# A DLRM tower on one core: the last tile's Gram matrix and first layer in two parts, and a later wait in the gather stream

## The reference

```python
combined = jnp.concatenate([dense_features[:, None, :], sparse_features], axis=1)   # (512, 27, 128)
interactions = jnp.einsum('bfd,bgd->bfg', combined, combined)
iu, ju = jnp.triu_indices(27, k=1)
z = jnp.concatenate([dense_features, interactions[:, iu, ju]], axis=1)
h = jnp.concatenate([z, dense_features], axis=1)          # 607 wide
h = jnp.maximum(h @ W_top1 + b_top1, 0.0)                 # 512
h = jnp.maximum(h @ W_top2 + b_top2, 0.0)                 # 256
y = h @ W_top3                                            # 1
```

## Time and profile before

| what | value |
|---|---|
| median of 3 runs | 140.15 us (139.18 to 140.3) |
| the profiled execution's own time | 141.27 us |
| its span, first to last instruction | 139.5 us |
| mean granted TensorE clock | 0.927 |
| TensorE busy | 116.3 us (83%) |
| VectorE, ScalarE busy | 79.1, 78.5 us |
| GpSimd busy | 69.8 us (50%) |

### The profile page before, as it was taken

The page is one execution under the profiler, slowest core; times in us unless marked ns, Lnnn a source line. Parts: engine busy times, 40 slices in busy tenths (PEclk is TensorE's granted clock), DMA queues, the critical chain, the costliest instruction groups (busy, mean ns, idle before and its releaser), DMA issues.

```text
span 139.5 us, 2681 instructions
## 1 busy us (share of the span) xinstructions
PE 116.3 (83%) x1038; PEld 97.9 (70%) x1038; DVE 79.1 (57%) x152; ACT 78.5 (56%) x157; POOL 69.8 (50%) x75
## 2 busy tenths in 40 slices
PE   0579999999999978783699876999559998929993
PEld 0347667667668646772699776999459997729992
DVE  3399999999999999397159212003931021860001
ACT  6985789699899861398159431232950312860021
POOL 2577570752783787676676775767767000000000
PEclk9999999999999999999569998699977999975799
DMA  4929767468698212121221221212212000000000
GB/s 145 259 56 276 234 162 215 136 146 250 155 341 269 55 38 56 42 56 45 62 63 42 59 66 40 56 42 56 61 38 56 19 0 7 0 0 5 0 0 1
DMA packets 6304, 12.58 MB, mean 90 GB/s; under 512 B 2545, under 2 KB 3157, under 8 KB 6163
## 3 DMA queue, kind: packets, MB, share of 16 engines
q1 hardware_dynamic: 3971, 7.68, 19.0%
q0 software_dynamic: 2176, 4.46, 12.3%
q10 hardware_dynamic: 144, 0.26, 0.7%
HBM read 11.27 MB, written 0.00 MB: 81 GB/s over the span
## 4 chain that ended last, share of the span: by engine, by line
DMA 36%; PE 31%; POOL 17%; issue 11%; DVE 4%; ACT 1%
DMA rows<-in_tbl_dram,ids_i 33%; POOL rows L336 17%; PE ps L595 16%; PE ps L566 4%; PE ps L606 4%; DVE z L480 4%; PE ps L517 3%; DMA ids_i<-in_ids_dram 2%; PE ps L550 2%; PE ps L616 1%; PE ps L614 1%; ACT y L423 1%; DVE h_t L489 0%
## 5 line engine op out<-in xcount | busy, mean ns | idle before, releaser
L336 POOL DMA_INDIRECT rows<-in_tbl_dram,ids_i x68 | 69.0, 1014 | 37.5 <-DMA rows<-in_tbl_dram,ids_i 20.0
L453 DVE TENSOR_SCALAR hot<-ps,row_no 125x512 fp32r<-125x512 f32 x54 | 36.6, 742 | 1.0 <-PE ps L504 1.0
L537 PE MATMUL ps<-hot,tab_lo 125*128 125x512 f32 x72 | 29.8, 414 | 1.7 <-DVE tab_lo L442 1.7
L534 PE MATMUL ps<-hot,tab_hi 125*128 125x512 f32 x72 | 30.5, 424 | 0.4 <-ACT emb_t L377 0.2
L480 DVE COPY z<-ps 32x112 f32<-32x112 f32 (+1 forms) x64 | 21.7, 340 | 12.2 <-PE ps L566 6.8
L404 ACT COPY z<-ps 32x112 f32<-32x112 f32 (+1 forms) x64 | 21.8, 341 | 11.8 <-PE ps L566 6.9
L566 PE MATMUL ps<-emb_t 128*64 128x52 f32 x512 | 18.2, 237 | 2.7 <-ACT emb_t L377 1.2
L566 PEld LDWEIGHTS ps<-emb_t 128*64 128x64 f32 x512 | 17.6, 154 | 3.9 <-ACT emb_t L396 2.0
L595 PE MATMUL ps<-z,w_pair 128*128 128x128 f32 (+1 forms) x112 | 17.9, 328 | 2.9 <-DVE z L480 2.9
L595 PEld LDWEIGHTS ps<-z,w_pair 128*128 128x128 f32 (+1 forms) x112 | 17.7, 244 | 3.3 <-ACT z L404 3.2
L411 ACT ACTIVATE h_t<-ps 128x128 f32<-128x128 f32 x16 | 4.3, 278 | 26.7 <-PE ps L595 26.7
(11 more groups left out here) (42 smaller groups left out, 88.8 us busy)
## 6 DMA issues: line engine op xcount, KB each, us to landing
tab<-in_tbl_dram SPq DMA_DIRECT2D x9, 448.0 KB
rows<-in_tbl_dram,ids_i POOLq DMA_INDIRECT x68, 2.6
w_fold<-w_pair SPq DMA_DIRECT2D x1, 1024.0 KB
w<-in_W_top_dram SPq DMA_DIRECT2D x1, 512.0 KB, 5.4
tab<-in_tbl_dram SPq DMA_DIRECT2D x9, 52.0 KB
x_rows<-in_r_dense_features_dram ACTq DMA_DIRECT2D x1, 256.0 KB, 3.1
w_x<-in_W_top_dram SPq DMA_DIRECT2D x1, 256.0 KB, 4.0
h_t<-in_W_top_dram SPq DMA_DIRECT2D x1, 256.0 KB, 4.4
```

The source lines that it names most:

```text
L336: pool.indirect_dma_start(out=rows[:, t, gathered.index(f), :], out_offset=None, in_=tables[f - 1], in_offset=bass.IndirectOffsetOnAxis(id ...
L453: nc.vector.tensor_scalar(hot[0:RP, k % OHB], ps[0:RP, IDV + n % 2, :], row_no[0:RP, c:c + 1], None, ALU.is_equal).then_inc(hot_dve, 1)
L534: nc.tensor.matmul(bank, tab_hi[0:RP, n % SPLIT, c], one_hot, start=c == 0, stop=False)
L537: nc.tensor.matmul(bank, tab_lo[0:RP, n % SPLIT, c], one_hot, start=False, stop=c == R8 - 1).then_inc(hot_used, 1)
```

## The change

Three things change together.

GROUPS is another partition of the same features: groups of 4, 4, 4, 3 and 3, in another order. The features 1, 2, 3 and 5, 6, 7 are now the last two groups. The wait of GpSimd stands ahead of a group's last gather, where it stood ahead of the second one.

For tile 3 (LAST) the Gram matrix is made in two parts, each over all 128 examples. The early part has the columns 8 to 25 (moving operand 36 wide), and it needs only the groups 0 to 2. The late part, the words v0 and v1 of ORDER, has the columns 0 to 7 (moving operand 16 wide), and it needs all. Each part has its own copies to z. The first layer of that tile is in two parts as well: mN does w_x and the five chunks of w_pair from column 8 up, and lN at the end the two chunks of columns 0 to 7. The four blocks then need four PSUM banks (block_ps). VectorE zeroes, with two more memsets before pads_ready, the slots of the features that the early part reads before they are there.

ORDER now gives a group's tile by name. The groups 3 and 4 of tile 3 go from the stage of tile 2 to the last stage. Of tile 0's groups ScalarE stores 0, 2 and 4, where it stored 1, 3 and 4.

```diff
-GROUPS = [[(0, 4)], [(12, 4)], [(5, 4)], [(9, 1), (19, 3)], [(23, 2)]]
+GROUPS = [[(12, 4)], [(8, 2), (23, 2)], [(0, 1), (19, 3)], [(1, 3)], [(5, 3)]]
+LATE = 8
+EARLY_GROUPS = 3
 ORDER = [
-    "h h g0 h g1 h g2 h g3 h g4 h h h",
-    "u0 g0 u1 g1 g2 g3 g4",
-    "u0-1 g0 x0 l0:0 l1:0 g1 l2:0 l3:0 g2 e0 g3 y0 x1 l0:1 l1:1 g4 l2:1 l3:1 e1",
-    "u0-1 y1 g0 x2 l0:2 g1 l1:2 g2 l2:2 g3 l3:2 e2 g4 y2",
-    "u0-1 x3 l0-3:3 e3 y3",
+    "h h g0:0 h g1:0 h g2:0 h g3:0 h g4:0 h h h",
+    "u0 g0:1 u1 g1-4:1",
+    "u0-1 g0:2 x0 l0:0 l1:0 g1:2 l2:0 l3:0 g2:2 e0 g3:2 y0 x1 l0:1 l1:1 g4:2 l2:1 l3:1 e1",
+    "u0-1 y1 g0:3 x2 l0:2 l1:2 g1:3 l2:2 l3:2 e2 g2:3 y2",
+    "u0-1 g3:3 m0-1 g4:3 m2 v0-1 m3 l0-3:3 e3 y3",
 ]
...
+        def columns(t, u):
+            if t < LAST:
+                return 0, NCOL
+            return (0, LATE) if u >= NU else (LATE, NCOL)
...
-                        if n == 1 and g:
+                        if n == len(fetched) - 1 and g:
                             pool.wait_ge(rows_in[t][g - 1], 16 * sum(a > 0 for a in features(GROUPS[g - 1])))
-                        elif n == 1 and t:
+                        elif n == len(fetched) - 1 and t:
                             pool.wait_ge(rows_in[t - 1][NG - 1], 16 * len(features(GROUPS[NG - 1])))
...
                         nc.vector.memset(emb_t[:, 2:, :, NF:], 0.0)
+                        for f0, n_late in [run for g in GROUPS[EARLY_GROUPS:] for run in g]:
+                            nc.vector.memset(emb_t[:, LAST, :, f0:f0 + n_late], 0.0)
...
-                                                    emb_t[:, t, b0:b0 + GT, 0:NCOL], start=True, stop=True)
+                                                    emb_t[:, t, b0:b0 + GT, c0:c1], start=True, stop=True)
...
+                elif s[0] == "l1_early":
+                    _, t, c = s
+                    if c == 0:
+                        pe.wait_ge(y_ready, t)
+                        wait_z(pe, (t + 1) * NU)
+                    nc.tensor.matmul(block_ps(t, c), w_x[:, c * P:(c + 1) * P], emb_t[:, t, :, 0], start=True, stop=False)
+                    for k in range(LQ, NQ):
+                        nc.tensor.matmul(block_ps(t, c), w_pair[0:depth(k), k, c * P:(c + 1) * P], z[0:depth(k), t % 2, k, :],
+                                         start=False, stop=False)
```

More of the change, by code:

```diff
@@ L49, in plan_steps @@
                 else:
-                    steps.append({"g": ("group", t + 1, n), "u": ("gram", t, n), "l": ("l1", int(tile or 0), n),
+                    steps.append({"g": ("group", int(tile or 0), n), "u": ("gram", t, n), "v": ("gram", t, n + 2),
+                                  "l": ("l1", int(tile or 0), n), "m": ("l1_early", t, n),
                                   "e": ("end", n), "y": ("y", n), "x": ("x", n)}[kind])
@@ L76, in dlrm_tower @@
     ND = 2
+    LAST = T - 1
+    LQ = LATE // 4
     ACT_CHUNKS = (3, 6)
@@ L229, in wait_z_free, with gram_at @@
             eng.wait_ge(l1_ps, (t - 1) * NB)
-        def z_copies(t, u):
-            bank = GRAM + 2 * (u % 2)
+        def columns(t, u):
+            if t < LAST:
+                return 0, NCOL
+            return (0, LATE) if u >= NU else (LATE, NCOL)
+        def gram_at(t, u, g):
+            c0, c1 = columns(t, u)
+            if u >= NU:
+                return GRAM + u % NU, g * GT * (c1 - c0)
+            return GRAM + 2 * u + g // BG, g % BG * GT * (c1 - c0)
+        def z_copies(t, u):
+            c0, c1 = columns(t, u)
+            wide = c1 - c0
+            bank = gram_at(t, u, 0)[0]
+            nb = gram_at(t, u, UG - 1)[0] - bank + 1
+            b0 = u % NU * UB
             for q in range(GB):
                 for r in range(4):
[L235 to L240, removed]
+                    own = q % GT * wide
+                    src = ps[32 * q:32 * q + SLOTS, bank:bank + nb, 0:UG // nb * GT * wide].rearrange(
+                        "p k (g c) -> p k g c", g=UG // nb)[:, :, :, own + r:own + wide:4]
+                    dst = z[32 * r:32 * r + SLOTS, t % 2, c0 // 4:c0 // 4 + len(range(r, wide, 4)), b0:b0 + UB].rearrange(
+                        "p n (k g b) -> p k g b n", k=nb, b=GB)[:, :, :, q, :]
                     yield q, src, dst
@@ L553, in _ @@
                     _, t, u = s
-                    if u == 0:
+                    if u % NU == 0:
                         if t == 0:
                             pe.wait_ge(pads_ready, 1)
-                        for b in [("group", t, g) for g in range(NG)] + [("hot", 0, NH - 1)]:
+                        groups = range(NG) if t < LAST else range(EARLY_GROUPS, NG) if u else range(EARLY_GROUPS)
+                        for b in [("group", t, g) for g in groups] + [("hot", 0, NH - 1)]:
                             wait_stored(pe, b)
@@ L586, in _ @@
                     cols = slice(c * P, (c + 1) * P)
-                    if c >= 2:
+                    if t == LAST:
+                        wait_z(pe, (t + 2) * NU)
+                    elif c >= 2:
                         x_part(t, c)
@@ L592, in _ @@
                         wait_z(pe, (t + 1) * NU)
-                    weights, nk = (w_fold, KF) if t < ND else (w_pair, NQ)
-                    for k in range(nk):
-                        last = nc.tensor.matmul(block_ps(c), weights[0:depth(k), k, cols], z[0:depth(k), t % 2, k, :],
-                                                start=False, stop=k == nk - 1)
+                    weights, chunks = (w_fold, range(KF)) if t < ND else (w_pair, range(LQ if t == LAST else NQ))
+                    for k in chunks:
+                        last = nc.tensor.matmul(block_ps(t, c), weights[0:depth(k), k, cols], z[0:depth(k), t % 2, k, :],
+                                                start=False, stop=k == chunks[-1])
                     last.then_inc(l1_ps, 1)
+                elif s[0] == "l1_early":
[3 more added lines that the diff above has]
+                        wait_z(pe, (t + 1) * NU)
+                    nc.tensor.matmul(block_ps(t, c), w_x[:, c * P:(c + 1) * P], emb_t[:, t, :, 0], start=True, stop=False)
+                    for k in range(LQ, NQ):
+                        nc.tensor.matmul(block_ps(t, c), w_pair[0:depth(k), k, c * P:(c + 1) * P], z[0:depth(k), t % 2, k, :],
+                                         start=False, stop=False)
                 elif s[0] == "end":
```

17 lines of the change are left out of this document (10 added, 7 removed).

## The result

The changed kernel takes **142.18 us** (median of 4, 142.06 to 143.33) against 140.23 for the kernel before on the same chip, a ratio of 1.018 (95% interval 1.011 to 1.025). Ratios and intervals here leave out executions in a slower state that every kernel has at times, such as one of 145.77 us of the kernel before. The change costs 2.0 us; the forecast was 139.8, and the range ended at 142.1. The profiled execution took 143.33 us with 141.2 of span, 2.06 more than the one before (141.27 and 139.5). It is the longest of those measured: its mean granted clock was 0.940, and that of the four others (142.06 to 142.23) 0.963. So its rows hold more low clock than the usual execution has, and where the others had less of it isn't known, as they left no trace.

A forecast was written before the change was run, and what follows sets the result against it. The prediction took TensorE's order, the z copies it awaits and its low clock behind gaps as the bound. Terms −2.95 + 0.1 − 0.66 + 3.2 = −0.31 us, from the median of 140.15, gave 139.8 us, range 137.6 to 142.1.

The forecast's parts named there:

- The gather stream, 2.95: Tile 1's stage: later wait removes the row wait at g3:2 (1.55 us) and keeps l0:1's clock up (1.4); gain 2.95 us.
- The rival of a low clock there: Tile 1's stage: the gap gets shorter but the clock falls all the same, costing 1.4 us (141.2); chance 0.15.
- The memsets, 0.1: VectorE ahead of pads_ready: two memsets of 0.34 us each move it from 55.84 to 56.5; loss 0.1 us, 0 to 0.2.
- Groups of two runs take two store copies, some tenths more, behind matmuls; no term: Stores of groups of two runs: the second copy takes some tenths more, hidden behind matmuls, so nothing was counted.
- The stage of tile 2, 0.66: Tile 2's stage loses the transposes of g3:3 and g4:3, six passes at 0.11 us, all on the path; gain 0.66 us.
- The last stage, 3.2: From tile 3's Gram matrix to e3: two parts take 21.2 us instead of 18.0; loss 3.2 us, 1 to 5.
- the 2.2 that stood for it: Last stage, m0 and m1: extra time taken for the low clock after the gap ahead of m0, 2.2 us.
- the 1.5 and 2.9 that gave the 2.2: Low clock's extra cost in the last stage if it covers 14 records (1.5 us) or 28 (2.9 us).
- The sum: Whole kernel: −2.95 + 0.1 − 0.66 + 3.2 = −0.31 us, from the median of 140.15 to 139.8 us.
- The sign that the clock's low stretches might lie otherwise: Whole kernel: the prediction falls if low-clock stretches lie elsewhere, each worth 1.5 to 3 us.
- The slow one, small copies at fixed cost: Last stage's z copies: small ones are all fixed cost, 0.33 us for a late copy; 2.3 us more, 142.1; chance 0.13.

## Why the prediction was wrong, step by step

- *The gather stream, 2.95:* right in the trace. The wait alone brought the last stage 2.91 forward, with 1.33 from the gap at g3:2 and 1.25 from the clock in l0:1 (1.4 expected); the other 0.3 stand ahead of both (l2:0's x at 77.52 for 77.82) and are not of the kind that was reckoned with. The rival of a low clock there did not come true.
- *The memsets, 0.1:* about right. They take 0.79 (0.68 expected), and the first Gram unit's weights load at 56.68 for 56.48.
- *"Groups of two runs take two store copies, some tenths more, behind matmuls; no term":* **this step failed.** The second copy is not behind matmuls: it stands on the path at the end of a gap, and costs 0.23 there. With what the clock and the z copies did behind it, the last stage started 0.86 later in the one pair of traces; how much of the other 0.6 is chance is open.
- *The stage of tile 2, 0.66:* **this failed too.** With memsets and low clock together, −0.56 was expected and +0.24 came (114.72 to 114.96). The transposes did leave, but the 28 records behind the gap took 5.53 us; with the groups alone 14 took 2.50 and 14 took 2.23, so 0.8 more. The prediction left the low clock behind this gap as long as it was before, where it covered the first 14 records, and so took its length from the one execution in hand, without a term or a rival for another. In four executions of the changed kernel the records took 4.18, 4.66, 5.39 and 5.53, and 5.74 with the last stage reordered.
- *The last stage, 3.2:* right in sum, 3.3, and in most of its parts: m0 at 6.93 behind the start (6.9), a gap of 2.52 (2.6), Gram units at one pace, late copies of 0.21, 21.3 in all (21.2). Its inner sizes were off against each other: m0 and m1 end 11.3 behind the start (11.75 expected) and the late Gram part 17.3 (17.4), so the low clock took less in m0 and m1 than the 2.2 that stood for it, g4:3 0.6 for 0.33, and m2 1.5 for 1.33; the l blocks took 2.0 for 1.78. That 21.3 came out so close is partly luck: the three further executions had 21.3 to 22.45, and the 1.5 and 2.9 that gave the 2.2 come to 1.3 and 3.0 by the rows they name.
- *The sum:* it was a difference of two terms of 3 us each, so 1.7 of error at the last stage's start, 0.1 in it, 0.2 behind it and 0.4 around the span turned −0.3 into +2.1. Of the 1.7, 0.86 came with the groups, the rest in tile 2's stage. The times, which hold more than one execution, divide it otherwise: wait and groups together won some 1.8 us (0.987) where 2.95 was reckoned, and memsets, tile 2's stage and the two parts cost 3.7 where 0.1 − 0.66 + 3.2 = 2.6 was, so each half was some 1.1 too good. The intervals are too wide to choose between the two.
- *The rivals:* none is what came. The sign that the clock's low stretches might lie otherwise did name the weak point, but no rival priced it for tile 2's stage. The slow one, small copies at fixed cost, gave the right time (142.1) by a wrong cause: a copy of 32 elements takes 0.21, not 0.33.

Shown by runs: that the two parts, and not the wait or the groups, make the changed kernel slower (142.18 against 138.46; a last stage of 21.2 to 22.45 against 16.5 to 17.9), and that filling the gaps is worth 4.3 us. Shown by one execution each: the wait's 2.91 at the last stage's start, the second copy's 0.23, tile 2's 5.53, and the 4.85 without low clock. Open: how the groups' 0.86 divides between the copy, the clock and chance, and which of these terms the usual execution at 142.1 had.

Two statements of the Trainium skill were weighed. "TensorE: Matmul & The Clock Gate", section "LDWEIGHTS (loading the stationary operand)": a load goes with its columns. Three widths of the moving operand at 0.030 us a record agree with that, but they would agree as well with a least time for a record, whatever its width: all have 64 stationary columns, and no run here changes that number. "VectorE: DVE Perf Modes", section "The TRN2 errata": the estimate of 0.16 us for a 32-element copy was too low; VectorE's took 0.209 us on average here, ScalarE's 0.212.

## What to carry over

Splitting the last unit of work, so that part of it runs early, pays only if the narrow part is cheaper; here 128 Gram records took the same time with 52, 36 and 16 moving columns, so the second part cost as much again, and it made new waits. Before any reordering look at what TensorE's clock does behind each gap: here idle matmuls in three gaps were worth 4.3 us, more than every reordering tried (the later wait brought 1.7 by its ratio and 2.9 in the trace). And where a forecast is the difference of two large terms, give the "some tenths" a term as well: the stores that end a gap are on the path even if they are hidden elsewhere.

## What the runs showed of the hardware

- What the low clock costs behind the same gap is not a constant: 28 records behind a gap of 3.1 to 3.4 us took 4.18 to 5.53 us in four executions of the changed kernel, and 3.30 in all four executions with the gap filled.
- TensorE's clock fell from 1.00 to 0.76 and 0.50 in a stretch in which it was 1.00 busy with 16-column Gram matmuls (186 to 189 us, above). Of 13 traces with the late Gram part, the clock fell in it or right behind it in five and stayed up in eight. Why is open.
- On three chips every kernel took about 190 us (medians 188.7 to 198), elsewhere 134 to 142. In the run of the kernel before with fill, TensorE's waits there (total us, times, longest) are

```profile
PE ps L566 <- issue: 39.7, 40, 2.6
```

  stops of up to 2.6 us between records of tile 0's Gram matrix, for which the profile names no releaser. In the changed kernel's first run on such a chip the time goes earlier, in the hot tables' part: one wait there is 34.3 us long and ends with a copy of ScalarE. This was not tried further, and its cause is open.
